# Attention of a decoder layer: softmax sums divided out after the output projection, value bias through the projection once, four-bank ring

## The reference, cut to what matters

```python
w = codes * jnp.repeat(scales, 32, axis=0)          # for wq, wk, wv, wo
q, k, v = x @ wq + bq, x @ wk + bk, x @ wv + bv     # 2 x 512 x 2048
attn = jax.nn.softmax(einsum('bqhd,bkhd->bhqk', q, k) / sqrt(128), axis=-1)
out = einsum('bhqk,bkhd->bqhd', attn, v)
x = layernorm(x + (out @ wo + bo))
x = layernorm(x + xattn(x, ctx))                    # top-54 of 1024 keys
x = layernorm(x + ffn(x))
```

## Time and profile before

| what | value |
|---|---|
| time, median of 3 runs (lowest to highest) | 983.53 us (982.94 to 984.64) |
| the profiled execution's own time | 983.78 us |
| its span, from the first instruction to the last | 981.9 us |
| mean granted TensorE clock, share of full speed | 0.99 |
| HBM read, mean over the span | 73.69 MB, 77 GB/s |

### The profile page before, as it was taken

The page is one execution under the profiler, slowest core; times in us unless marked ns, Lnnn a source line. Parts: engine busy times, 40 slices in busy tenths (PEclk is TensorE's granted clock), DMA queues, the critical chain, the costliest instruction groups (busy, mean ns, idle before and its releaser), DMA issues.

```text
span 981.9 us, 13037 instructions
## 1 busy us (share of the span) xinstructions
PE 926.3 (94%) x4498; PEld 753.3 (77%) x4498; DVE 648.4 (66%) x1264; ACT 555.4 (57%) x1147; POOL 398.5 (41%) x315
## 2 busy tenths in 40 slices
PE   9999899999999989999998989979999899999997
PEld 7777677777777767777776878878878788788886
DVE  5787867777768787777787599894768414521114
ACT  4665765566756667566776456453473743443333
POOL 4345330343212414252533355651674662354440
PEclk9999999999999999999999999979999999999999
DMA  6531220122200212121221122330443251253331
GB/s 194 151 107 44 86 82 1 49 65 70 82 17 27 81 48 81 49 67 53 75 63 58 53 77 66 116 99 16 134 119 97 76 160 34 64 151 97 97 86 43
DMA packets 46099, 76.95 MB, mean 78 GB/s; under 512 B 5584, under 2 KB 11216, under 8 KB 45776
## 3 DMA queue, kind: packets, MB, share of 16 engines
q1 hardware_dynamic: 45600, 75.68, 26.2%
q10 hardware_dynamic: 432, 0.39, 0.2%
HBM read 73.69 MB, written 2.36 MB: 77 GB/s over the span
## 4 chain that ended last, share of the span: by engine, by line
PE 69%; DVE 20%; issue 4%; ACT 3%; POOL 2%; DMA 1%; POOLq 0%; ACTq 0%; DVEq 0%
PE p L99 65%; DVE JK L443 4%; DVE PT L480 3%; PE p L470 3%; DVE PR L461 2%; DVE QK L363 2%; DVE acc L429 2%; DVE OT L500 1%; POOL RAW L274 1%; DVE WV L278 1%; DVE st L532 1%; PE p L723 1%; DVE m L670 0%; DMA SCL<-in_sq 0%; DMA SCL<-rq 0%
## 5 line engine op out<-in xcount | busy, mean ns | idle before, releaser
L443 DVE TENSOR_SCALAR_CACHE_REDUCE JK<-p,ssc 128x512 bf16<-128x512 f32 x112 | 83.8, 748 | 98.2 <-PE p L99 98.1
L598 POOL TENSOR_TENSOR V<-RAW,V 128x512 fp32r<-128x512 f32 x64 | 81.7, 1295 | 142.5 <-ACT V L597 142.5
L99 PE MATMUL p<-R 128*128 128x512 f32 x544 | 135.6, 392 | 0.6 <-DVE R L521 0.6
L451 ACT ACTIVATE PR<-p,nms,ssc 128x512 f32<-128x512 f32 x112 | 87.2, 779 | 78.4 <-DVE JK L443 78.0
L99 PE MATMUL p<-QK 128*128 128x512 f32 x384 | 117.7, 415 | 7.4 <-DVE QK L363 6.8
L99 PEld LDWEIGHTS p<-R 128*128 128x128 f32 x544 | 101.6, 188 | 23.4 <-DVE R L521 1.0
L99 PE MATMUL p<-R,V 128*128 128x512 f32 x480 | 112.6, 390 | 0.7 <-ACT C L597 0.7
L278 POOL TENSOR_TENSOR R<-RAW,R 128x512 fp32r<-128x512 f32 x36 | 48.5, 1348 | 156.7 <-ACT R L275 156.7
L99 PEld LDWEIGHTS p<-R,V 128*128 128x128 f32 x480 | 89.9, 188 | 19.8 <-issue 1.1
L274 POOL TENSOR_TENSOR RAW<-RAW,SCL 128x512 f32<-128x512 f32 x65 | 85.9, 1336 | 37.3 <-DMA SCL<-in_so 20.4
L831 DVE TENSOR_TENSOR SX<-p,SX 128x512 f32<-128x512 f32 x32 | 22.1, 692 | 115.7 <-PE p L99 109.0
(11 more groups left out here) (162 smaller groups left out, 1636.0 us busy)
## 6 DMA issues: line engine op xcount, KB each, us to landing
RAW<-in_wg SPq DMA_DIRECT2D x32, 256.0 KB, 2.9
RAW<-in_wu SPq DMA_DIRECT2D x32, 256.0 KB, 2.7
RAW<-in_ctxn SPq DMA_DIRECT2D x32, 256.0 KB, 2.9
RAW<-in_wd SPq DMA_DIRECT2D x32, 256.0 KB, 2.9
RAW<-in_wq SPq DMA_DIRECT2D x19, 256.0 KB, 2.9
RAW<-in_wk SPq DMA_DIRECT2D x18, 256.0 KB, 2.7
RAW<-in_wv SPq DMA_DIRECT2D x16, 256.0 KB, 2.8
RAW<-in_wo SPq DMA_DIRECT2D x16, 256.0 KB, 3.1
```

The lines of the kernel that those rows point to most:

```text
L99: return e.matmul(outp, a, b, start=st, stop=sp_)
L443: tm = op(dve, lambda e: e.tensor_scalar(JK[:, :], ps, nsc, None, ALU.mult, ALU.min, accum_out=m), T[("S", i)], T.get(("max", i - 1)), T.g ...
L451: T[("exp", i)] = op(act, lambda e: e.activation(PR[:, i % 3, :], ps, ACT.Exp, bias=m, scale=sc, accum_out=rs[:, i % 4:i % 4 + 1]), T[("ma ...
L598: tl = op(pool, lambda e: e.tensor_tensor(lo, raw, hi, ALU.subtract), th, free)
```

## The change

1. The probabilities are no longer multiplied by the reciprocals. `norm` goes; `transp` waits for the exponential; `recip` runs once a head over four columns. PR has two buffers instead of three.
2. `proj_o` uses one bank for each of the two heads, each with its own branch, and scales it by the reciprocal while adding: the first head's bank by one DVE operation straight into `acc`, queued at once; the second's by a copy with scale on ACT into one of two buffers and an addition on POOL, for pairs up to 12, and by DVE again from pair 13 on.
3. `av` is evacuated without bias. `bias_o` multiplies the value bias (hi and lo as two columns) with WO, for two pairs of heads at a call, four calls; `bias_row` spreads the sum to all partitions and makes it the content of `BO`; the additions of `BO` to `acc` for it (`add_bo`) come at i = 115 to 122, besides those of the output bias, which stay.
4. The ring has four banks (4 to 7); `av` and `bias_o` take theirs from it.
5. A weight piece has three stages: loads and multiplication in one step, hi in the next (`halves`), lo in the one after (`flush`). The Q and K pieces start one step earlier (qt 1 and 2). Flags have four columns in turn instead of eight; `run_sums` comes after the evacuations and not in step 0.
6. The first layer norm's statistics start one step later, at (29, 1).

The diff, cut to its core:

```diff
-        bv_t = sbt(top, "bv_t", [128, 16])
+        bv_r = sbt(top, "bv_r", [128, 16, 2], F32R)
...
-        PR = sbt(ph1, "PR", [128, 3, 512])
+        PR = sbt(ph1, "PR", [128, 2, 512])
+        CB = sbt(ph1, "CB", [128, 512])
...
             tm = op(em, lambda e: e.tensor_tensor(rv, rv, sv_, ALU.mult), td, ts)
-            th = op(act, lambda e: e.activation(hi, raw, ACT.Copy), tm, free)
-
-            def b():
+            def a():
+                th = op(act, lambda e: e.activation(hi, raw, ACT.Copy), tm, free)
+                pend.append(lambda: b(th))
+
+            def b(th):
                 tl = op(el, lambda e: e.tensor_tensor(lo, raw, hi, ALU.subtract), th, free)
...
-            pend.append(b)
+            if own is None and not pre:
+                half.append(a)
+            else:
+                a()
+
+        def halves():
+            while half:
+                half.pop(0)()
...
-            k = nf[0] % 3
+            k = nf[0] % 4 - 1
             nf[0] += 1
             return k, P[5 + k][:, :]
...
         def proj_o(q, tt):
-            k, ps = fbank()
             h, b = HB[2 * q]
-            p = h // 2
-            pairs, extra = [], []
+            p, r = h // 2, b * 4 + tt
+            a, c = acc[:, r], slice(tt * 128, (tt + 1) * 128)
+            f, t_f = flag_of(("o", p))
             for i in range(2):
                 j = 2 * q + i
-                c = slice(tt * 128, (tt + 1) * 128)
-                pairs += two(OT[:, j % 4, 0, c], OT[:, j % 4, 1, c], WO[:, p % 2, i, 0])
-                extra.append((OT[:, j % 4, 0, c], WO[:, p % 2, i, 1]))
-            f, t_f = flag_of(("o", p))
-            t = mm_if(ps, pairs, extra, "o", f, None if tt else t_f, W[("o", p)], T[("ot", 2 * q)], T[("ot", 2 * q + 1)],
-                      bank[5 + k])
+                k, ps = fbank()
+                pairs = two(OT[:, j % 4, 0, c], OT[:, j % 4, 1, c], WO[:, p % 2, i, 0])
+                extra = [(OT[:, j % 4, 0, c], WO[:, p % 2, i, 1])]
+                t = mm_if(ps, pairs, extra, "o", f, None if tt or i else t_f, W[("o", p)], T[("ot", j)], bank[5 + k])
+                s = ri[:, 4 * (j % 4) + tt:4 * (j % 4) + tt + 1]
+                if i and q < 13:
+                    n = 4 * q + tt
+                    buf = SX0[:, (n % 2) * 512:(n % 2 + 1) * 512]
+                    ts = op(act, lambda e, ps=ps, s=s, buf=buf: e.activation(buf, ps, ACT.Copy, scale=s), t,
+                            T[("rec", j)], T.get(("add", n - 2)), T[("scr", 0)], T[("scr", 1)])
+                    bank[5 + k] = T[("scaled", j)] = ts
+
+                    def add_(ts=ts, buf=buf, n=n):
+                        T[("add", n)] = T[("acc", r)] = T[("add",)] = op(
+                            pool, lambda e: e.tensor_tensor(a, buf, a, ALU.add), ts, T[("acc", r)])
+                else:
+                    def add_(t=t, ps=ps, s=s, k=k, j=j):
+                        bank[5 + k] = T[("scaled", j)] = T[("acc", r)] = op(dve, lambda e: e.scalar_tensor_tensor(
+                            out=a, in0=ps, scalar=s, in1=a, op0=ALU.mult, op1=ALU.add), t, T[("rec", j)], T[("acc", r)])
+                if i and q < 13:
+                    evac.append(add_)
+                else:
+                    add_()
...
+        def bias_o(p0):
+            k, ps = fbank()
+            o = ps[0:2, :]
+            first = True
+            for p in (p0, p0 + 1):
+                f, t_f = flag_of(("o", p))
+                hs = [bv_r[:, 2 * p + i, :] for i in range(2)]
+                mm(o, [(hs[0], WO[:, p % 2, 0, 0])], W[("o", p)], T[("bv",)], bank[5 + k] if first else None,
+                   start=first, stop=False, count=False)
+                pe.add(lambda e, f=f: e.load(regs["b"], f), flat([t_f]), False)
+                first = False
...
+                t = mm(o, [(hs[1], WO[:, p % 2, 1, 0])], start=False, stop=p > p0)
...
+        def bias_row():
+            k, ps = fbank()
+            t = pe.add(lambda e: e.matmul(ps, ones[0:2, 0:1].to_broadcast((2, 128)), CB[0:2, :], start=True, stop=True),
+                       flat([T[("cb",)], t_one, bank[5 + k]]), True)
+            T[("cbrow",)] = t
+            bank[5 + k] = T[("borow",)] = op(act, lambda e: e.activation(BO[:, :], ps, ACT.Copy), t, T[("bo",)])
...
-        def recip(i):
-            T[("rec", i)] = op(dve, lambda e: e.reciprocal(ri[:, i % 4:i % 4 + 1], rs[:, i % 4:i % 4 + 1]),
-                               T[("exp", i)], T.get(("norm", i - 4)))
-
-        def norm(i):
-            p = PR[:, i % 3, :]
-            T[("norm", i)] = op(dve, lambda e: e.tensor_scalar(p, p, ri[:, i % 4:i % 4 + 1], None, ALU.mult),
-                                T[("rec", i)])
+        def recip(j):
+            T[("rec", j)] = op(dve, lambda e: e.reciprocal(ri[:, 4 * (j % 4):4 * (j % 4) + 4],
+                                                           rs[:, 4 * (j % 2):4 * (j % 2) + 4]),
+                               [T[("exp", 4 * j + q)] for q in range(4)], T.get(("scaled", j - 4)))
...
-                           flat([T[("norm", i)], free, t_id]) if kt == 0 else [], kt == 3)
+                t = pe.add(lambda e, c=c: e.transpose(tp[:, c], PR[:, i % 2, c], ident[:, :]),
+                           flat([T[("exp", i)], free, t_id]) if kt == 0 else [], kt == 3)
...
-            ps = P[4][:, :]
-            t = mm(ps, pairs, T[("v", G, b)], [T[("Tev", 4 * j + q)] for q in range(4)], T.get(("ot", j - 1)))
+            k, ps = fbank()
+            t = mm(ps, pairs, T[("v", G, b)], [T[("Tev", 4 * j + q)] for q in range(4)], bank[5 + k])
...
-            if i + 1 < 4 * NJ:
-                recip(i + 1)
+            if qt == 3:
+                recip(j)
             if qt < 2 and j + 1 < NJ:
                 proj_qk(j + 1, qt)
-            if i + 1 < 4 * NJ:
-                norm(i + 1)
...
-            run_sums()
             evacs()
+            if qt:
+                run_sums()
+            if j % 8 == 6 and qt == 1 and j < 24 or i == 112:
+                bias_o((j - 6) // 4 if j < 24 else 6)
+                evacs()
...
-            if qt >= 2 and j + 3 < NJ and WJ[j + 3] == j + 3:
-                todo.append(lambda: prep_qk(j + 3, qt - 2))
+            if qt in (1, 2) and j + 3 < NJ and WJ[j + 3] == j + 3:
+                todo.append(lambda: prep_qk(j + 3, qt - 1))
...
-            if not todo:
-                flush()
+            flush()
+            halves()
             for f in todo:
                 f()
-                while len(pend) > 1:
-                    pend.pop(0)()
...
+            if i == 114:
+                bias_row()
+            if 115 <= i <= 122:
+                add_bo(i - 115, T[("borow",)], T[("acc", i - 115)])
...
-            if (j, qt) == (29, 0):
+            if (j, qt) == (29, 1):
                 ln_stats([0, 1])
```

More of the change, by code:

```diff
@@ L208, in decoder_layer @@
         pend = []
+        half = []
         NJ = 32
@@ L245, in run_sums @@
                 o = ps[0:1, 0:n]
-                t = pe.add(lambda e, o=o, col=col, n=n: e.matmul(o, ones[:, 0:1], mag[:, col % 8, 0:n],
+                t = pe.add(lambda e, o=o, col=col, n=n: e.matmul(o, ones[:, 0:1], mag[:, col % 4, 0:n],
                                                                  start=True, stop=True),
@@ L356, in evac_qk @@
             T[("proj", j, w)] = t
-            bias = (bqs if h > 1 else bqk_t)[:, w * 16 + h:w * 16 + h + 1]
+            bias = bqk_t[:, w * 16 + h:w * 16 + h + 1]
             hi, lo = QK[:, s, w, 0], QK[:, s, w, 1]
@@ L423, in proj_o, with low @@
+                if i and q < 13:
+                    evac.append(add_)
+                else:
+                    add_()
             if tt == 3:
                 T[("woproj", p, b)] = T[("otfree", q)] = t
-            a = acc[:, b * 4 + tt]
-            def add_():
-                r = b * 4 + tt
-                ta = op(dve, lambda e: e.tensor_tensor(a, ps, a, ALU.add), t, T[("acc", r)])
-                bank[5 + k] = ta
-                T[("acc", r)] = ta
-            evac.append(add_)
+        def bias_o(p0):
[9 more added lines that the diff above has]
+                first = False
+                def low(e, hs=hs, p=p):
+                    with e.If_ne(regs["b"], 0):
+                        for i in range(2):
+                            e.matmul(o, hs[i], WO[:, p % 2, i, 1], start=False, stop=False)
+                pe.add(low, [], False)
+                t = mm(o, [(hs[1], WO[:, p % 2, 1, 0])], start=False, stop=p > p0)
+            def add_():
+                c = CB[0:2, :]
+                if p0 == 0:
+                    t2 = op(dve, lambda e: e.tensor_copy(c, o), t, T["vs"])
+                else:
+                    t2 = op(dve, lambda e: e.tensor_tensor(c, o, c, ALU.add), t, T[("cb",)])
+                bank[5 + k] = T[("cb",)] = t2
+            evac.append(add_)
@@ L490, in av @@
                 pairs += three(V[:, b, 0, kt, c], V[:, b, 1, kt, c], PT[:, 0, kt], PT[:, 1, kt])
-            ps = P[4][:, :]
```

(28 more changed lines are left out.)

25 lines of the change are left out of this document (13 added, 12 removed).

## The result

The kernel after takes 974.93 us (median of 5 runs, 973.57 to 975.85) where the kernel before takes 983.64 (5 runs beside it): a ratio of 0.9902, 95% interval 0.9882 to 0.9923, so 8.7 us faster, 978.1 forecast. The profiled execution took 973.63 us, its span is 971.8, that of before 981.9.

The account below looks back on a forecast made before the run. PE's queue was taken as the bound (busy 926.3 of 981.9 us), its attention waits all for DVE. Gains and losses on waits and added work summed to -5.7 from 983.78, so 978.1 us; range 966 to 988, 972 to 981.5 at 0.50.

Parts of the forecast that it names:

- ring, regular heads: Attention stage: with four PSUM banks, output projections no longer wait for the add into acc; 7 us gained, bounds 3 to 9.1.
- normalization: Attention steps: transposes follow the exponential directly, so PE's 11 waits for DVE's softmax scaling go; 8 us gained, bounds 6 to 8.8.
- QK: Attention stage: PE's 13 waits for DVE's low-half subtraction shorten, 5.2 of 8.4 us staying; 3.2 gained, bounds 2 to 8.4.
- ACT's lateness: Short heads with weight pieces: added copies make ACT finish late, delaying AV and the flag's matmul; 3.8 us lost, bounds 0 to 10.
- three calls of the bias there: Value bias through the output projection on PE: four calls cost 5.9 us in all, bounds 3.6 to 7.7; three fall here, +4.4.
- the wait at 522.30: End of attention stage: PE's 2.27 us idle for the QK subtraction halves, clock may recover; 2 us gained, bounds 0 to 4.
- tail: After attention, DVE is the path: four tiles take two scaled additions instead of one; 2.4 us lost, bounds 1 to 3.5.
- A: Rival, short heads: ACT becomes the bound, its copies standing ahead of the exponential and lag carrying over; 991 us, chance 0.14.
- B: Rival, output projections: 64 extra branches at 0.204 us are not hidden behind matmuls; +13 us, 991 us, chance 0.05.
- D: Rival, attention stage: QK waits vanish too and ACT keeps up, eight heads taking below 125 us; 968 us, chance 0.14.
- C: Rival, PE's waits: a third of the 18 us gained is paid again at ACT's checks and QK subtraction; 984 us, chance 0.17.
- The three stages: Weight pieces: high copy one step later, so ACT need not stand behind POOL's multiply; nothing gained or lost, within 1 us.

Follow-up runs that it names:

- ring alone: The kernel before with only its PSUM bank ring changed, four banks with AV's among them instead of three: 972.29 us, ratio 0.9890 to before.
- the waited multiplication: The kernel after plus a DVE multiplication by one of the probabilities every step, where the normalization stood, transposes waiting for it: 1001.18 us, ratio 1.0184 to before.
- the kernel with two stages: The kernel after with each weight piece's high copy issued in the same step as its multiplication, low half a step later: 1025.69 us, ratio 1.0418 to before.

## Why the prediction came out as it did

**Against its own sum.** Faster was right, and 974.9 lies in the forecast's own band of 972 to 981.5. The profiled spans differ by 10.1 us, and the stretches take that apart:

| term | forecast | measured | from |
|---|---|---|---|
| ring, regular heads | -7 | -9.5 | ring alone against before |
| normalization, QK, ACT's lateness | -8 -3.2 +3.8 = -7.4 | -7.1 | after without bias against ring alone, regular heads |
| three calls of the bias there | +4.4 | +1.9 | after against after without bias |
| last block: bias, row, two additions, the wait at 522.30 | +1.5 +0.9 +1.5 -2 = +1.9 | +2.4 | after against before |
| tail | +2.4 | +2.7 | after against before |
| up to head 2 | 0 | -0.4 | |

Of the difference of 4.4 between -5.7 and -10.1, the ring and the bias make 2.5 each; the other rows take 0.6 back.

**The ring** was right in kind and too small in size. I had taken off 2 us for a new wait of the second value projection of a long head; the list of PE's waits after has no line for V, and the long heads without a call for the bias are 16.4 to 16.9 us, near the 16.82 of the undisturbed one in the earlier trace rows. The 9.5 is the ring's price in the kernel before; taken out of the kernel after, where a head takes more banks, it costs 17.4. Part of the term for the wait at 522.30 is the ring's too: with the ring alone the last block is already 1.4 us shorter, and its clock 1.00 where before had 0.98. In the kernel after that wait is 1.18 (at 510.18), half as long, as forecast. But `av` of head 29 stands 1.79 for PT (at 500.07), which the sum did not have.

**The normalization's row** (-7.1 for -7.4) is right in part by luck. Between its two kernels, in the regular heads and with the 0.16 of each record, the waits for the normalization fall by 8.4 us (8 forecast), those for QK by 0.2 (3.2), and those at the weight pieces, for PT, the checks and an issue behind them, grow by 2.8 (3.8); the rest, about 1, stands in no such wait. Set back into the kernel after, the multiplication costs 26 us and not 8, 22 of them with nobody waiting for it. So its removal also made room on DVE, which the first halves' additions took up: as I read it, the change is one trade, and neither half of it has a price of its own. The step that failed is the one that costs each edit against the old queue and adds them.

**QK**: the single wait is as forecast, 0.25 idle and 0.16 for the record, 0.41, where 0.40 was said to stay. The sum is not: from 44 to 505 us there are 15 such waits and not 13, one of them 0.9, so 6.8 us stay where 5.2 were forecast, and 1.6 are won and not 3.2. **ACT's lateness** shows where I put it, at the three heads with value pieces: PT 0.45, the check 0.77, an issue behind it 0.19, with the records 1.9 a head and 5.7 in all, where I had 8.

**ACT as the bound** (A) did not come: its sign, PE waiting for the exponential, is 0.7 us in the list. Moving the copies to DVE makes the kernel 22 us slower; that shows DVE to be the worse place, and not what the copies cost on ACT. The rule of the Trainium skill (ScalarE: Activation LUTs, Rules for kernel authors) to give multiplications and additions to VectorE would have cost some 2% here. The measurement decides: with 0.680 on ACT against 0.734 on DVE the tile is no dearer on ACT, and DVE's queue is where PE's next matmul waits. **The branches** (B) are refuted by the kernel without 64 of them. **D**'s mark, a round of eight heads below 125 us, was passed (244.76 to 369.15, 124.39), but by the ring and the bias, not as D said: the QK waits stayed. **C** holds in small part: 14.0 us of idle time went with acc and the normalization, and about 3 came back, 1.9 of them at the checks, while the waits for QK fell.

**The bias** was priced as added work on a busy engine. Beside each regular call, however, PE would have stood about 0.5 us for the QK subtraction, and the call fills that (all of it at the first two calls, 0.30 at the third): the head with a call is 18.62 to 18.98 us, without it 17.99 to 18.04, so 0.6 to 0.9 a call where I had 1.47. I had looked for cover for the branches inside the call and not for a wait that the call covers. And the eight additions of the output bias do not move, as I wrote: they stay, and eight more of 1.29 us come on POOL. With the row, whose matmul takes PE 1.1 us, and the last call they cost 1.1 in the last block, where I had 2.4.

**The three stages** were put at "nothing gained or lost, within 1 us". As a difference from before this may hold; no run prices it. But I had named what they do, that ACT need not stand behind POOL's multiplication, and seen a detail where it is the change's condition. I had named POOL's 68 us of additions as lying beside an engine with room, and not asked what else is queued on POOL, and who waits behind ACT for that. Without the three stages the kernel is 42 us slower than before.

**The tail** was right within 1 us: its beginning loses 3.2 for 2.4, and normalising the last heads brings just that back.

## What to carry to other kernels

Where each tile takes a fixed round of PSUM banks, count who frees the bank that comes next: one bank more, from a buffer that stood apart, won here by itself no less than the whole change (11.7 and 8.7 us in the medians), in half a dozen lines. An operation that is moved to a little-used engine puts its time into that engine's order too; look for what is queued behind it and which busier engine waits for that, and move that wait a step later. And where an engine's queue is full in a step, removing an operation and adding another there are one term, not two.

## What the runs showed of the hardware

One multiplication of 128x512 from SBUF to SBUF on DVE takes 0.479 us in the median and up to 1.635, the subtraction with an operand in PSUM never more than 0.693. The lines (least, median and most ns), first from the kernel with the waited multiplication, then from the kernel after:

```profile
L524 DVE TENSOR_SCALAR PR<-PR,ones x128: 454/479/1635, 21.9 to 568.2; 128x512 f32<-128x512 f32 x128
```

```profile
L538 DVE TENSOR_TENSOR PT<-p,PT x128: 679/682/693, 33.5 to 548.1; 128x512 fp32r<-128x512 f32 x128
```

In the timeline above the one of 1.42 us overlaps a multiplication of POOL. All 45 of the 128 that took over 0.6 us overlap an instruction of POOL; 64 of the 128 subtractions overlap one too, and are no longer for it. The Trainium skill (SBUF — State Buffer, SBUF: two separate sides) says that DVE in its fast modes and POOL take turns at one pair of ports, for whole instructions; the rows agree that they get in each other's way, and do not show whether for whole instructions. With POOL at 479 us busy instead of 399 the mean of this operation in the attention stage is 0.775 where the normalization had 0.672 in the kernel with the ring alone.

PE's clock fell at a long wait: in the kernel with two stages `av` starts at 270.42 after 3.58 us idle, and the granted clock, 1.00 in the stretch before, is 0.50 (1.2 of 2.4 GHz) in the next 3.6 us. Not every such wait does this: at 407.05 in the same profile `av` starts after 3.57 us idle, and the clock stays at 1.00.

```profile
262.00:266.80 4.80, 4.80 (x24) 3.42 (x23) 4.34 (x10) 4.09 (x12) 2.61 (x2) 1.00 0.25 68
270.42:274.00 3.58, 3.58 (x9) 2.81 (x10) 0.00 (x0) 2.37 (x7) 3.53 (x3) 0.50 0.23 61
...
407.05:410.65 3.60, 3.60 (x18) 3.01 (x19) 0.00 (x0) 2.95 (x9) 3.57 (x3) 1.00 0.04 3
```

Over the regular heads of the kernel with two stages the clock is 0.96, so a part of the 51 us is this and not the waits themselves.
